# Warm-up matmuls, an early exponential and two more context buffers in a cross-attention and FP8 feed-forward kernel

## The reference

```
# x: 4 x 512 x 512, ctx: 4 x 512 x 256 (float32)
q = ctx @ Wq.T + bq ;  k = ctx @ Wk.T + bk          # 4 x 512 x 128
att = softmax(q @ k.T)                              # 4 x 512 x 512, over the last axis
x = x + layernorm(x) @ att.T
# mxq: per block of 32 values a scale max|t|/448, values rounded to fp8 e4m3 and scaled back
n = mxq(layernorm(x))
h = silu(n @ mxq(gate_w).T) * (n @ mxq(up_w).T)     # inner size 2048
out = x + mxq(h) @ mxq(down_w).T
```

## Time and profile before

| | us |
|---|---|
| median of 3 runs | 623.9 (623.51 to 624.44) |
| profiled execution | 624.55 |
| its span | 622.8 |
| TensorE busy in the span | 597.6 (96%) |
| VectorE busy | 514.7 (83%) |
| ScalarE busy | 268.3 (43%) |
| GpSimd busy | 39.4 (6%) |

### The profile page before, as it was taken

The page is one execution under the profiler, slowest core; times in us unless marked ns, Lnnn a source line. Parts: engine busy times, 40 slices in busy tenths (PEclk is TensorE's granted clock), DMA queues, the critical chain, the costliest instruction groups (busy, mean ns, idle before and its releaser), DMA issues.

```text
span 622.8 us, 7023 instructions
## 1 busy us (share of the span) xinstructions
PE 597.6 (96%) x2560; PEld 269.9 (43%) x2560; DVE 514.7 (83%) x516; ACT 268.3 (43%) x341; POOL 39.4 (6%) x50
## 2 busy tenths in 40 slices
PE   4899988799999999999999999999999999999997
PEld 1344434344444444444444444444444444444443
DVE  3899999799989989889898996888189459978941
ACT  1798976554462444553424323422132133424310
POOL 0000110010100000200000000000000001000100
PEclk9999989899999999999999999999999999999999
DMA  8839979667999585655603008400540197157780
GB/s 346 349 77 219 278 234 266 157 147 188 199 193 271 128 203 140 138 107 106 144 2 68 0 1 152 86 1 0 85 85 1 30 139 149 35 119 138 116 137 35
DMA packets 146433, 82.05 MB, mean 132 GB/s; under 512 B 134112, under 2 KB 134112, under 8 KB 142688
## 3 DMA queue, kind: packets, MB, share of 16 engines
q1 hardware_dynamic: 142512, 64.30, 43.8%
q0 software_dynamic: 3888, 17.30, 13.0%
HBM read 26.02 MB, written 8.39 MB: 55 GB/s over the span
## 4 chain that ended last, share of the span: by engine, by line
PE 83%; DMA 7%; SPq 5%; DVE 3%; ACT 1%; issue 1%; DVEq 0%; ACTq 0%; POOLq 0%
PE G L696 54%; PE A L711 27%; SPq L363 3%; DMA W<-hT 3%; DMA gu_hi<-hT 2%; DMA xT<-hT 1%; SPq L358 1%; PE A L674 1%; PE A L653 1%; DMA gu_hi<-in_ctxT 1%; DVE W L1407 1%; ACT hT L876 1%; PE G L661 0%; DVE W L1300 0%; DVE W L1288 0%
## 5 line engine op out<-in xcount | busy, mean ns | idle before, releaser
L696 PE MATMUL G<-gu_hi,xT 128*128 128x512 f16 x1024 | 307.5, 380 | 3.7 <-issue 3.7
L696 PE MATMUL G<-gu_lo,xT 128*128 128x512 f16 x512 | 194.6, 380 | 0.0
L711 PE MATMUL A<-dn,hT 128*128 128x512 f16 x768 | 167.2, 379 | 0.0
L696 PEld LDWEIGHTS G<-gu_hi,xT 128*128 128x128 f16 x1024 | 100.4, 98 | 126.6 <-issue 6.7
L970 ACT ACTIVATE silu<-G,unscale 128x512 f32<-128x512 f32 x64 | 43.9, 686 | 167.1 <-PE G L696 149.2
L711 PEld LDWEIGHTS A<-dn,hT 128*128 128x128 f16 x768 | 75.1, 98 | 90.8 <-issue 0.4
L696 PEld LDWEIGHTS G<-gu_lo,xT 128*128 128x128 f16 x512 | 50.3, 98 | 60.7 <-issue 1.0
L1448 DVE SCALAR_TENSOR_TENSOR h<-G,unscale,silu 128x512 f32<-128x512 f32 x64 | 46.7, 738 | 20.6 <-PE G L696 20.0
L674 PE MATMUL A<-dn,h 128*128 128x512 f32 x128 | 57.9, 609 | 4.1 <-ACT dn L931 3.2
L1502 DVE SCALAR_TENSOR_TENSOR W<-h,W 128x2048 f16<-128x2048 f32 x15 | 34.3, 2284 | 24.4 <-DMA hT<-W 19.7
L1283 DVE SCALAR_TENSOR_TENSOR h<-mag,h 128x2048 f32<-128x2048 bf16 x18 | 41.1, 2283 | 10.4 <-ACT mag L863 10.4
(11 more groups left out here) (90 smaller groups left out, 452.0 us busy)
## 6 DMA issues: line engine op xcount, KB each, us to landing
W<-in_units SPq DMA_DIRECT2D x12, 1024.0 KB, 6.3
W<-hT POOLq DMA_DIRECT2D x11, 1024.0 KB, 6.0
h<-in_xcols SPq DMA_DIRECT2D x4, 1024.0 KB, 11.8
out_y<-y POOLq DMA_DIRECT2D x14, 256.0 KB, 5.3
h<-in_xrows SPq DMA_DIRECT2D x3, 1024.0 KB, 6.2
out_y<-h SPq DMA_DIRECT2D x3, 1024.0 KB, 8.8
gu_hi<-in_ctxT SPq DMA_DIRECT2D x4, 512.0 KB, 9.0
W<-out_y SPq DMA_DIRECT2D x2, 1024.0 KB, 6.1
```

The lines of the kernel that those rows point to most:

```text
L696: last = pe.matmul(dst[:, :], xT[:, b % 2, part, k, :], w[:, c, g, j * 512:(j + 1) * 512], start=(m == 0), stop=(m == 3 * HT - 1))
L711: last = pe.matmul(bank[:, :], hT[:, r % 2, a, k, :], dn[:, w, k, :], start=(m == 0), stop=(m == 3 * IT - 1))
```

## The change

Three things are added or altered.

1. VectorE first writes zeros to `zeros`, 128 x 512 f16 in the place of the transposed rows `xT[:, 0, 0]`, which is filled much later. TensorE begins its list with `warm_up`: it waits for the zeros and does 12 matmuls of 128 x 128 by 128 x 512 on them into the PSUM bank `G[0]`; nobody reads the result.
2. ScalarE begins its list with an exponential of 128 x 4 zeros into `sums`, which nobody reads.
3. Every context has a buffer and a semaphore of its own. Contexts 2 and 3 lie in `gu_hi[:, 2]`, the place of units 4 and 5. `load_ctx` no longer waits for anything; instead the transposes of units 4 and 5 (`unit_place`) wait until all eight projections are done.

```diff
+    WARM_UPS = 12
...
-        ctx_all = gu_hi[:, CH - 1, :, :].rearrange("p g n -> p (g n)").bitcast(F32)
-        ctx = [ctx_all[:, n * 1024:(n + 1) * 1024].rearrange("p (t n) -> p t n", n=512) for n in range(2)]
+        ctx = [gu_hi[:, CH - 1 - n // 2, n % 2, :].bitcast(F32).rearrange("p (t n) -> p t n", n=512) for n in range(B)]
...
+        zeros = xT[:, 0, 0, 0:4, :].rearrange("p k n -> p (k n)")
...
+        zeros_ready = sem("zeros_ready")
-        ctx_in = [sem(f"ctx_in{k}") for k in range(2)]
+        ctx_in = [sem(f"ctx_in{b}") for b in range(B)]
...
             def load_ctx(b):
-                if b >= 2:
-                    sp.wait_ge(proj_ready, 2 * (b - 1))
-                sp.dma_start(ctx[b % 2], ctx_cols[b]).then_inc(ctx_in[b % 2], 16)
+                sp.dma_start(ctx[b], ctx_cols[b]).then_inc(ctx_in[b], 16)
...
             def unit_place(u):
+                if u in (U_GU - 4, U_GU - 3):
+                    sp.wait_ge(proj_ready, 2 * B)
                 if u >= U_GU - 2:
...
         def _(pe):
+            def warm_up():
+
+                pe.wait_ge(zeros_ready, 1)
+                for _ in range(WARM_UPS):
+                    pe.matmul(G[0][:, :], zeros[:, 0:P], zeros[:, :], start=True, stop=True)
...
             def project(b, i):
                 bank = take_bank(f"j{b}.{i}")
-                pe.wait_ge(ctx_in[b % 2], 16 * (b // 2 + 1))
+                pe.wait_ge(ctx_in[b], 16)
                 for t in range(CT):
-                    last = pe.matmul(bank[:, :], (wq, wk)[i][:, t, :], ctx[b % 2][:, t, :],
+                    last = pe.matmul(bank[:, :], (wq, wk)[i][:, t, :], ctx[b][:, t, :],
                                      start=(t == 0), stop=(t == CT - 1))
...
+            warm_up()
             pe.wait_ge(consts_in, 16)
...
+            act.wait_ge(zeros_ready, 1)
+            nc.scalar.activation(sums[:, :], zeros[:, 0:LT], ACT.Exp)
             act.wait_ge(consts_in, 16)
...
+            dve.memset(zeros, 0.0).then_inc(zeros_ready, 1)
             first_stats(0, 0)
```

## The result

The changed kernel takes 625.84 us in the median of 20 executions (624.3 to 627.68), the kernel before 624.02 in 20 beside it (621.86 to 625.15): a ratio of 1.0031, with an interval of 1.0022 to 1.004. The change makes the kernel slower by about 1.8 us. The prediction said 623.9 and a range up to 625.3: the measured time is 1.9 us above the first and 0.5 us above the second. Of the later executions of the changed kernel one (in e15) took 1289.38 us; it stands in no median here.

The account below looks back on a forecast made before the run. Bound by TensorE from 112.64 us, ahead of it by a serial chain from unit_hi(0); the 3.0 us lead ends at context 2's wait, so 624.55 + 0.0, less 0.65, gives 623.9 us, range 622.5 to 625.3.

Parts of the forecast that it names:

- The lead of 3.06 us: Context 0's eight projection passes run at TensorE's upper level, so its energies come at 12.47 us, 3.06 us earlier.
- Warm-ups, memset and exponential: At the kernel's start, before context 0 lands at 7.97 us: hidden in idle time, costing nothing.
- rival Z: Warm-ups don't raise the level before 8.10 us, or it falls again before the first projection: unchanged, 623.9 us; chance 0.15.
- The exponential: Moves ScalarE's 1.28 us table load to idle time; worth 0.2 to 0.3 us with faster projections, outside the sum.
- The contexts' earlier issue: Loads of contexts 2 and 3 issued earlier on SyncE keep their place in the queue: worth 0 us.
- The case F: Clock falls during the longer wait for context 2, cancelling the lead at unit_hi(0): 623.9 us, likeliest, chance 0.45.
- the price of the fall: Effect on unit_hi(0) of slow passes after context 2's wait: 0 in the middle, from 0.3 us earlier to 0.4 later.
- F2: The lower level lasts for all eight passes at project(2, 0), take_projection(2, 1) 2.1 us later: 626.0 us; chance 0.10.
- N: The clock holds through the wait for context 2, unit_hi(0) at 34.9 us: gain 1.24 us, 622.7 us; chance 0.22.
- Bound by TensorE behind 112.64: From 112.64 us to the end only TensorE's matmuls count, so time is won only by arriving there earlier.
- The rope: Serial chain from unit_hi(0) at 36.14 us through transposing DMAs to product(0, 0) at 112.64, passing any gain on.

Follow-up runs that it names:

- e15: The whole change unaltered, profiled for one more trace; that execution took 627.03 us.
- e2: The kernel before with the zeros and 12 warm-up matmuls alone: 625.21 us, 1.0028.
- e4: The whole change with context 2 loaded ahead of columns 1 and context 3 ahead of rows 2: 623.96 us, 0.9995.
- e8: The whole change with contexts 2 and 3 loaded ahead, and GpSimd's second_norm(1) moved behind unit_rest(4): 630.5 us, 1.0099.
- e6: The kernel before with 12 dummy matmuls between attend(3, 1) and product(0, 0): 624.32 us, 1.0006.
- e5: The whole change with 10 more matmuls of zeros between turn_probs(0, 0) and project(2, 0): 622.35 us, 0.9977.
- e1: The whole change unaltered, measured once more: 625.53 us, 1.0028.
- e9: The whole change with 16 warm-ups instead of 12 and 10 matmuls of zeros ahead of project(2, 0): 622.49 us, 0.9964.
- e10: The whole change unaltered, profiled for one more trace; that execution took 625.02 us.
- e12: The whole change unaltered, profiled for one more trace; that execution took 624.37 us.
- e7: The kernel before with GpSimd's second_norm(1) moved behind unit_rest(4): 633.02 us, 1.0138.
- e3: The kernel before with the four context buffers alone: 624.51 us, 1.0011.
- e16: The whole change unaltered, profiled for one more trace; that execution took 626.04 us.
- e11: The whole change unaltered, profiled for one more trace; that execution took 625.15 us.

## Why the prediction was wrong

**The lead of 3.06 us** was half of that. Warm-ups, memset and exponential cost nothing, as said: the memset took 0.27 us (0.3 taken) and the matmuls ended at 5.56 (6.2 at the latest). But the prediction let the level hold from there to 8.10, and gave its fall only a place in the rival Z. It fell at this wait, 1.9 to 2.6 us long, in all seven traces of the whole change, where the passes took 5.1 to 5.4 us, and did not in e2, where the warm-ups ended later and the wait was 1.69. The truth lay between Z and the step: a lead of 1.1 to 1.7 us at the energies. For the time this step was not the one that failed, as the lead ends at context 2.

**The exponential** hid what it was said to hide: the activation starts 1.30 us behind the load again (0.72 and 2.02). In e2, which lacks it, the load lies at 10.22, and TensorE waits 0.98 us instead of 0.78 ahead of the energies: 0.20 us, where 0.2 to 0.3 were estimated.

**The contexts' earlier issue** was worth 0, as worked out. SyncE issued both at 12.26, context 2 in 16.09 us landed at 28.35, and the eight projections found it at 28.5 to 29.0 in every trace. Only another order in the queue moved it (e4).

**The case F** was the likeliest one and its mechanism came out: in seven of seven traces the level fell at that wait. The Trainium skill's rule in "TensorE: Matmul & The Clock Gate", section "HAM oscillation — how this bites in real kernels", says that waits for DMA between bursts let the clock fall back; the traces of the whole change agree, seven of seven, and e2 with 3.87 us of waiting doesn't. The step that failed is the size of one term, the price of the fall: 0 in the middle, from -0.3 to +0.4 us at `unit_hi(0)`. Against the 36.14 of the one trace it was -0.1 to +0.6 in six traces and +1.7 in the seventh. The long fall, F2, was put at one in ten, on the ground that both falls of the trace had cost 1.7 us and no more; it was seen in one trace of seven and ends at 627.03, where the range took in only the half of it. That the profiled execution, with 36.22 and 624.3 us, lies so near to F's 624.55 is luck: it was the shortest of the twenty.

**From trace to median.** The prediction took the 0.65 us between the profiled run and the median of before off the forecast too, as if both kernels had that slack. The starts of the other kernels with before's beginning (35.63, 35.74, 36.31) put a typical one at 35.96: against it the fall costs 0.7 us in the mean and not 0. The prediction named that correction for N, where it reduces a gain, and left it out for F, where it makes a loss. The other half of the 1.35 us between the medians, and with it a part of why the time came out above 625.3, is explained by no run.

**"Bound by TensorE behind 112.64"** failed as a reading. The hole of 0.18 us at 199.06 in the earlier trace rows was taken for nothing; it is the place where TensorE waits for unit 7. The wait there is 0.18 to 2.02 us in the traces (e8 has none), and e6 shows that a faster product gains nothing because of it. The rope therefore doesn't end at 112.64 but at the transposes near 194. It is not rigid either: between `unit_hi(0)` and unit 7's low transpose it took from 157.8 to 160.1 us.

## What to carry to other kernels

In this kernel, warming TensorE up moved the slow passes to the end of the next wait for a DMA. Filling that wait as well made it a gain (e5: 0.9977 where the warm-ups alone gave 1.0028); reordering the loads so that the wait is not there took the loss away (e4: 0.9995). An engine that arrives earlier at a fixed landing wins nothing there, and may resume slower. And a tiny hole in a busy engine's chain deserves a look at what released it: what stands behind it can be a second bound with next to no slack, and what the engine alone gains ahead of it is lost there (e6).

## What the runs showed of the hardware

- The level fell at idle times as short as 1.90 us (e1, ahead of context 0) and 1.91 us (e9, ahead of context 2), and held over one of 3.87 us (e2), in programs that differ little. Between project(2, 1) and project(3, 0) the same idle time of 2.11 us went without a fall in e4 and with one in e8. So the length of a wait alone didn't decide it.
- The granted clock fell as early as 0.6 us before TensorE resumed (e10, ahead of context 2) and as late as 1.0 us behind it (e1 and e12, at context 0): a wait can be followed by one or two fast passes before the slow ones.
- At the start of the kernel the granted clock stands at 1.00 while passes of 512 columns take 0.85 us each (before, 8.10 to 14.75). There the level is read from the passes and not from that column.
- After a fall the sixteen f32 passes took 8.5 to 8.8 us in six traces of the whole change and in e7 and e9, and 10.18 us in one, against 7.10 us at the upper level.
- GpSimd shows 7.3 to 10.3 us without any record between its all-reduce or accumulating DMA and a power of 128x4 values that itself takes 1.05 to 2.6 us; the stretch follows the power when that is moved (e7).
- From `unit_rest(3)` to `unit_rest(4)` GpSimd took 18.10 us in the five traces in which the first product fell to the lower level (before, e3, after, e10, e16), and 19.96 to 20.6 us in the eleven in which it did not (e1, e2, e4, e5, e6, e9 and e11 to e15; e7 and e8 have another order there). From the start of `unit_hi(0)` to the end of the execution both kinds take the same, 588.7 and 588.5 us in the mean, so it isn't a loss. Only e6 set this on purpose; why a slower TensorE goes with a shorter step is open.
- The same transpose held SyncE's queue for either 9.3 to 9.9 us or 10.3 to 10.7 us.
